# One set of input, staging and sum buffers for all stages, with each stage loading ahead for the next

## The reference

```python
h = layernorm(x)
x1 = x + cross_attention(h, ctx)            # 16 heads of 32, softmax over 154 rows
y = layernorm(x1)
for l in range(2):                          # two layers
    h = shift_token(y)                      # columns 256..511 come from the token before
    q, k, v = split(h @ wqkv[l])            # 8 heads of 64; q and k l2-normed, rotated
    y = y + local_attention(q, k, v) @ wo[l]    # window of 256, looks one window back
    h = layernorm(shift_token(y)) * lg[l] + lb[l]
    a, g = split(h @ w1[l] + b1[l])         # hidden size 1365
    y = y + (a * gelu(g)) @ w2[l] + b2[l]
return x1 + y
```

## Time and profile before

| what | value |
|---|---|
| median of 3 runs | 3664.63 us (3656.72 to 3667.29) |
| the profiled execution | 3661.59 us, its span 3659.8 us |
| mean granted clock | 0.977 |
| TensorE busy | 3448.6 us, 94% of the span |
| VectorE, ScalarE, GpSimd busy | 2278.2, 1502.2, 1138.6 us |
| DMA | 223.00 MB, 61 GB/s on average |

### The profile page before, as it was taken

How to read it: one execution, slowest core, us unless ns; L and a number is a source line. 1 busy time by engine, 2 the same in 40 slices (tenths; PEclk the granted TensorE clock), 3 DMA queues, 4 the chain that set the end, 5 groups by cost and what they waited for, 6 DMA issues and landing times. The chain is left out here.

```text
span 3659.8 us, 56458 instructions
## 1 busy us (share of the span) xinstructions
PE 3448.6 (94%) x20560; PEld 2796.4 (76%) x20560; DVE 2278.2 (62%) x5002; ACT 1502.2 (41%) x3975; POOL 1138.6 (31%) x1004
## 2 busy tenths in 40 slices
PE   5999995999999979999999979999999699999999
PEld 4667664888888867888888858888888578888887
DVE  5788875899999974333332249999999542323332
ACT  4666663555555543111111135555555321111111
POOL 2443432555565520000000035555555111111111
PEclk7999997999999999999999989999999899999999
DMA  5022224111111123111111021112111231111111
GB/s 134 14 71 63 70 60 140 47 59 59 59 59 59 59 80 96 43 43 43 43 43 43 31 95 59 59 59 69 60 60 53 88 110 48 43 38 49 47 48 37
DMA packets 201262, 223.00 MB, mean 61 GB/s; under 512 B 33286, under 2 KB 139022, under 8 KB 200987
## 3 DMA queue, kind: packets, MB, share of 16 engines
q1 hardware_dynamic: 200987, 219.38, 19.1%
HBM read 129.78 MB, written 69.64 MB: 54 GB/s over the span
## 5 line engine op out<-in xcount | busy, mean ns | idle before, releaser
L1741 DVE SCALAR_TENSOR_TENSOR u_full<-banks,b_cols,gate 128x512 f32<-128x512 f32 (+1 forms) x176 | 132.1, 751 | 888.0 <-ACT gate L1682 801.2
L46 PE MATMUL banks<-fxT_h,w_h 128*128 128x512 f32 (+1 forms) x1408 | 558.3, 396 | 8.0 <-DVE fxT_l L1733 5.0
L48 PE MATMUL banks<-fxT_h,w_l 128*128 128x512 f32 (+1 forms) x1408 | 557.4, 396 | 0.0
L47 PE MATMUL banks<-fxT_l,w_h 128*128 128x512 f32 (+1 forms) x1408 | 556.6, 395 | 0.0
L1682 ACT ACTIVATE gate<-banks,b_cols 128x512 f32<-128x512 f32 (+1 forms) x176 | 121.2, 689 | 1021.3 <-PE banks L48 1021.3
L1578 POOL TENSOR_TENSOR f_res<-f_res,b_rows 128x512 f32<-128x512 f32 x64 | 86.1, 1377 | 827.4 <-DMA f_res<-z_rows 827.4
L1027 POOL TENSOR_TENSOR rn<-ssq,neg_half 128x8 f32<-128x8 f32 x128 | 211.6, 1653 | 410.4 <-DVE ssq L1299 404.0
L46 PE MATMUL banks<-wqkv_h,hT_h 128*128 128x512 f32 x768 | 322.7, 420 | 15.1 <-DVE wqkv_l L1286 15.1
L46 PEld LDWEIGHTS banks<-fxT_h,w_h 128*128 128x128 f32 (+1 forms) x1408 | 260.4, 185 | 79.9 <-DVE fxT_l L1733 12.3
L1340 DVE TENSOR_SCALAR prob<-prob,rc 128x384 f32<-128x384 f32 (+2 forms) x512 | 315.4, 658 | 9.1
L1235 ACT ACTIVATE pT_h<-banks 128x384 fp32r<-128x384 f32 (+2 forms) x512 | 213.8, 469 | 256.0 <-PE banks L1124 254.7
(11 more groups left out here) (178 smaller groups left out, 8188.7 us busy)
## 6 DMA issues: line engine op xcount, KB each, us to landing
y_in<-y_rows SPq DMA_DIRECT2D x64, 256.0 KB, 2.9
z_rows<-y_in SPq DMA_DIRECT2D x64, 256.0 KB, 2.0
f_res<-z_rows SPq DMA_DIRECT2D x16, 1024.0 KB, 5.5
w_ffn_stage<-in_w SPq DMA_DIRECT2D x30, 512.0 KB, 5.4
x_in<-in_x SPq DMA_DIRECT2D x10, 1024.0 KB, 6.8
x_rows<-x_in SPq DMA_DIRECT2D x8, 1024.0 KB, 4.3
y_rows<-y_t SPq DMA_DIRECT2D x8, 1024.0 KB
h_in<-y_rows SPq DMA_DIRECT2D x64, 128.0 KB, 2.7
```

What stands on the lines that cost most here:

```text
L46: pe.matmul(out, a_h, b_h, start=start, stop=False)
L47: pe.matmul(out, a_h, b_l, start=False, stop=False)
L48: return pe.matmul(out, a_l, b_h, start=False, stop=stop)
L1741: e.scalar_tensor_tensor(out=u_full[r, m % 2, :], in0=ps[r, 2 * (m % 2), :], scalar=b1[r, place[m], 0:1], in1=gate[r, :], op0=ALU.add, op1 ...
```

## The change

One buffer `thirds` (three groups wide) serves as `x_in` of cross attention, and for all later stages its first two thirds are the weight stage and its last third the input tiles `h_in`. One buffer `sums` serves as `y`, `y_in` and `res`. The small tensors of the feed-forward stage are allocated once. Each stage, before it ends, issues on SP the first loads of the next: cross attention three input tiles and 4 of 8 pieces, attention group 0, four small tensors and 4 pieces, the feed-forward stage of layer 0 three tiles and 8 pieces. The statistics and the normalising of group 0 move into attention's last tile, the root to the end of GpSimd's stream. Row `N` is no longer overwritten: the store that would reach it is cut to 127 rows, once in cross attention, in each attention stage and in the feed-forward stage of layer 0. The waits for the stores at the end of a stage move to the next stage's first load of a sum. Cross attention's two unread reloads of x, the statistics of one of them, the second reload of keys and values, and the key copies of attention's last turn go. TensorE's first hidden block waits for one k of the input at a time.

```diff
+    thirds = ctx.enter_context(nc.sbuf_tensor("thirds", [P, XSLOTS, GT, D], F32))
+    stage = thirds[:, 0:2].rearrange("p s t d -> p (s t d)")
+    h_in = thirds[:, 2]
+    sums = ctx.enter_context(nc.sbuf_tensor("sums", [P, GT, D], F32))
+    X_PIECES = SLOTS["w_attn"] // 2
...
+def load_piece(e, s, w, n):
+    e.wait_ge(s["w_lo"], w.freed(n))
+    e.dma_start(w.staged(n), w.src(n)).then_inc(s["w_ld"][n % w.slots], 16)
...
 def cross_phase
-                        e.dma_start(x_in[:, g.slot(2)], src).then_inc(ld_x[g.slot(2)], 16)
+                    if it + 2 < NG:
+                        e.wait_ge(st_x1, 16 * it)
+                        e.dma_start(x_in[:, g.slot(2)], rows(io["x"], (it + 2) * G)).then_inc(ld_x[g.slot(2)], 16)
...
+                        e.dma_start(late[:, 0:GT - 1], y[:, 0:GT - 1, HALF:D]).then_inc(st_y, 16)
+                        e.dma_start(late[0:P - 1, GT - 1], y[0:P - 1, GT - 1, HALF:D]).then_inc(st_y, 16)
...
-                    if s == XSLOTS - 1:
+                    if g.it == SECOND - 1:
...
                 run(e, body)
+                e.wait_ge(st_x1, 16 * (NG - 2))
+                e.wait_ge(st_y, 32 * (NG - 3) + 16)
+                for t in range(3):
+                    load_tile(e, ahead["s"], ahead["h_in"], ahead["dram"], t)
+                e.wait_ge(st_x1, 16 * (NG - 1))
+                for n in range(ahead["pieces"]):
+                    load_piece(e, ahead["s"], ahead["w"], n)
                 store_before(Group(NG, NG, 0), NG)
                 e.wait_ge(st_x1, 16 * NG)
-                e.wait_ge(st_y, 32 * NG)
-                for s in range(XSLOTS):
-                    e.wait_ge(ld_x[s], 16 * len(range(s, NG + 1, XSLOTS)))
-                e.dma_start(dram["late"][N:N + 1, :], zero_row[:]).then_inc(st_y, 16)
-                e.wait_ge(st_y, 32 * NG + 16)
...
 def attention_phase
+                        n = P - 1 if ends_sequence(r + P) else P
+                        e.dma_start(dram["dst_late"][bass.ds(r2, n), :], y_in[0:n, j % 4, HALF:D]).then_inc(s["st"][j % 4], 16)
...
+                        if (i, u) == (0, 0):
+                            dram["is_stored"](e)
                         e.wait_ge(s["st"][u], 32 * (l * NI) + i * 32)
...
+                        if i == NI - 1 and u == 2:
+                            e.wait_ge(s["pe_h"], at(NT, NI, 4, 0))
+                            ffn_load_in(e, ahead["s"], ahead["t"], ahead["dram"], 0)
+                            ffn_load_small(e, io, ahead["s"], ahead["t"], l)
+                            e.wait_ge(w_lo, w.done(w.count))
+                            for n in range(w_next.slots):
+                                load_piece(e, ahead["s"], w_next, n)
-                        if u >= 2:
+                        if u >= 2 and i < NI - 1:
...
-                load_h(0, 0)
-                load_weights(0, w.slots)
+                load_weights(dram["pieces"], w.slots)
...
-                load_h(0, 1)
                 load_weights(w.slots, w.count)
-                load_h(0, 2)
...
                 store(NI - 1, 3)
-                e.wait_ge(s["k_copy"], 64 * (l * NI) + 64 * NI)
-                for u in range(4):
-                    e.wait_ge(s["st"][u], 32 * (l * NI) + 32 * NI)
-                e.dma_start(dram["dst_late"][N:N + 1, :], zero_row[:]).then_inc(s["ld_small"], 16)
-                e.wait_ge(s["ld_small"], 16 * 8 * l + 16 * 8)
...
                 for i in range(NI):
                     body(i)
+                ffn_root(e, ahead["s"], ahead["t"], l, 0)
...
+                        if (t, p) == (NT - 1, 0):
+                            ffn_moments(e, ahead["s"], ahead["t"], l, 0)
+                        if (t, p) == (NT - 1, 2):
+                            ffn_normalise(e, ahead["s"], ahead["t"], l, 0)
...
 def ffn_phase
-                load_in(0, None)
...
-                load_weights(0, 4 * PAIR)
+                e.dma_start(b2[:], io["b2"][bass.ds(l, 1), :].to_broadcast([P, D])).then_inc(s["ld_b2"], 16)
+                load_weights(w.slots, 4 * PAIR)
                 for g in range(NG):
+                    if is_last(g) and ahead:
+                        e.wait_ge(s["pe_x"], at(DC, NG, 0))
+                        for t in range(3):
+                            load_tile(e, ahead["s"], ahead["h_in"], ahead["dram"], t)
+                        e.wait_ge(s["w_under"], 32 * l + 32)
+                        for n in range(ahead["pieces"]):
+                            load_piece(e, ahead["s"], ahead["w"], n)
                     body(g)
-                e.wait_ge(s["st"], stored(NG))
-                if not ends:
-                    e.dma_start(dram["dst_late"][N:N + 1, :], zero_row[:]).then_inc(s["ld_small"], 16)
-                    e.wait_ge(s["ld_small"], 16 * SMALL * l + 16 * SMALL)
+                if ends:
+                    e.wait_ge(s["st"], stored(NG))
...
-                    if m == 0:
-                        e.wait_ge(s["dv_x"], at(DC, g, DC))
...
+                        if is_first(g) and m == 0:
+                            e.wait_ge(w_lo, w.done(x + 1))
                         for k in range(DC):
+                            if m == 0 and x == 0:
+                                e.wait_ge(s["dv_x"], at(DC, g, k + 1))
...
-                round_weights(0, 2)
+                round_weights(0, 1)
                 for k in range(DC):
                     affine(0, k)
-                round_weights(2, PAIR)
+                round_weights(1, PAIR)
...
-                normalise(0, lambda: rest_of_weights(0, 1))
-                rest_of_weights(1, 2)
+                rest_of_weights(0, 1)
                 for k in range(DC):
                     split_x(0, k)
-                rest_of_weights(2, PAIR)
+                rest_of_weights(1, PAIR)
```

More of the change, by code:

```diff
@@ L51, with __init__ @@
 class Pieces:
-    def __init__(self, stage, slots, pieces, l=0):
-        self.stage, self.slots, self.pieces, self.count = stage, slots, pieces, len(pieces)
+    def __init__(self, stage, slots, rows, l=0):
+        self.stage, self.slots, self.rows, self.count = stage, slots, rows, len(rows)
+        self.parts = None
         self.before = l * self.count
@@ L60, in src @@
     def src(self, n):
-        return self.pieces[n][0]
+        return self.rows[n]
     def staged(self, n):
-        shape = self.pieces[n][0].shape
+        shape = self.rows[n].shape
         at = self.stage[0:shape[0], n % self.slots, 0:int(np.prod(shape[1:]))]
@@ L395, in store_before @@
                     r, r_late = g.row(e, -1), g.row(e, -1, 1)
-                    if it is g.it and not g.last:
-                        src = rows(io["x"], (it + 2) % NG * G)
                     e.wait_ge(dv_x1, GT * it)
@@ L566, in reloaded @@
                     def reloaded(half, loaded):
[L568 to L569 removed]
+                        if it == SECOND:
+                            e.wait_ge(half, 2 * loaded)
                     for q in range(DC):
@@ L808, in body @@
                                     finish(it - 1, g.slot(-1), tt)
-                            if (q, k) in ((DC - 1, 2), (DC - 1, 4)) and not g.last:
+                            if (q, k) in ((DC - 1, 2), (DC - 1, 4)) and it + 2 < NG:
                                 moments(g.slot(2), g.round(2), (0, 1) if k == 2 else (2, 3))
-                    assert g.last or own[0] == (OWN_FIRST if g.first else OWN), own[0]
+                    assert it + 2 >= NG or own[0] == (OWN_FIRST if g.first else OWN), own[0]
                 moments(0, 0, range(GT))
@@ L849, in attention_sems, with attention_pieces, weight, load_tile @@
     return s
-def attention_phase(nc, io, ps, ident, s, neg_half, l, dram, zero_row):
+def attention_pieces(io, stage, l):
+    def weight(name):
+        src = io[name].rearrange("l k n -> (l k) n")
+        return [src[bass.ds(l * D + k * P, P), :] for k in range(DC)]
+    return Pieces(stage.rearrange("p (s d) -> p s d", d=D), SLOTS["w_attn"],
+                  [a[:, j * D:(j + 1) * D] for j in range(3) for a in weight("wqkv")] + weight("wo"), l)
+def load_tile(e, s, h_in, dram, t):
+    e.dma_start(h_in[:, t % 4, 0:HALF], dram["src"][bass.ds(t * P, P), 0:HALF]).then_inc(s["ld_h"][t % 4], 16)
+    e.dma_start(h_in[:, t % 4, HALF:D], dram["src_late"][bass.ds(t * P, P), :]).then_inc(s["ld_h"][t % 4], 16)
+def attention_phase(nc, io, ps, ident, s, neg_half, l, h_in, y_in, w, dram, ahead):
     LH = NT * HEADS
@@ L1424, in ffn_sems, with ffn_pieces @@
     return s
-def ffn_phase(nc, io, ps, ident, s, neg_half, l, dram, zero_row):
+def ffn_pieces(io, stage, l):
+    src1 = io["w1"].rearrange("l k n -> (l k) n")
+    src2 = io["w2"].rearrange("l k n -> (l k) n")
+    pieces = []
+    for c0 in range(0, HID, 2 * P):
+        n = min(2 * P, HID - c0)
+        for x in range(2):
+            pieces.append(src1[bass.ds(l * D, D), x * HID + c0:x * HID + c0 + n].rearrange("(k p) c -> p k c", p=P))
+        rows = src2[bass.ds(l * HID + c0, n), :]
```

(28 more changed lines are left out.)

200 lines of the change are left out of this document (92 added, 108 removed).

## The result

The changed kernel takes **3604.01 us** (median of 4 runs, 3602.36 to 3604.46) against 3663.23 for the kernel before (4 runs, 3656.72 to 3667.29): a ratio of 0.9839, 95% interval 0.9822 to 0.9856. That is 59 us less; 3605 was predicted, 3593 to 3618 the range. The profiled execution has a span of 3602.7 us (before 3659.8), so its 57.1 us are what the traces can account for.

A forecast was written before the change was run, and what follows sets the result against it. TensorE sets the time, so its idle waits at stage openings (38.3 and 29.7 us) can be won: 14.6 + 10.3 + 16.4 + 18.2 + 0.5 = 60.0 us off the profiled 3661.6, plus 3.0 to the median, gives 3605 us, range 3593 to 3618.

The forecast's parts named there:

- Restart: Hand-over between stages: the next stage starts 0.4 us after SP reaches its end, between 0.2 and 1.28.
- Cross attention to attention: Hand-over into attention of layer 0: 12.8 us from the earlier start plus 1.8 in the opening, 14.6 us won.
- the opening's 1.8: Attention's opening in layer 0: piece 8 issued 5.8 us after the transposes instead of 7.1, 1.8 us won in all.
- Feed-forward to attention of layer 1: Hand-over into attention of layer 1: 8.2 us from the earlier start plus 2.1 in the opening, 10.3 us won.
- Attention to feed-forward: Hand-overs into the feed-forward stage: first gate 12.5 us after the restart; net 16.4 us won in layer 0, 18.2 in layer 1.
- The 11 that I had worked out: Feed-forward opening: the second 12 matmuls end about 11 us after the restart at 2.4 GHz, about 14 at 1.2.
- The last tile: Attention's last tile: the added statistics and normalising cost 1.9 us in layer 0 and 0.5 in layer 1.
- Rest: Unread loads and one set of statistics dropped: 0.5 us won, bounds 0 to 2; the 127-row stores 0.
- the one with the clock held: Rival: shorter gaps keep the clock up, 11 us at both feed-forward openings, 9 us more won, 3596; chance 0.13.
- the other rival: Rival: low clock at feed-forward openings and a dearer last tile, where the clock falls, lose some 15 us, 3620; chance 0.13.
- The signs: Expected TensorE waits: near 2 us before the 16 transposes, 7 and 2 before attention's; first gates 14 us after attention's last matmul.
- one of the bad ones: Sign against the forecast: pieces 4 to 7 late after cross attention, behind 1.5 MB of y stores, costing up to 2 us.

The follow-up runs named there:

- the end waits back: Changed kernel with SP's wait for the landing of the last stores back at each stage's end, all loads ahead kept: 3612.62 us.
- the padding of 1696 bytes: Changed kernel with 1696 bytes of padding ahead of attention's buffers, making their shift a multiple of 2048: 3598.72 us.

## Why the prediction was right, and where it was not

**Restart, 0.4 us.** Right: 0.44 after attention, 0.65 after cross attention, 0.59 after the feed-forward stage.

**Cross attention to attention, 14.6.** Measured 12.2. The shift is right, 13.0 (609.76 to 596.76) for 12.8. The step that failed is the opening's 1.8, which came out as a loss of 0.8: from the transposes to the first residual it is 67.3 us, against 66.5 before. Piece 8 was to be issued 5.8 us after the transposes and went out after 7.5, because SP issues slower while 1.5 MB of stores are in flight. With the stores landed (the end waits back) it goes out after 5.4 and the multiply comes after 15.4 us instead of 17.1, which is 1.6 us earlier than before the change and close to what was forecast. Moving piece 8 alone could give 1.5 us at most, since the root on GpSimd is done only 1.5 us before the multiply. The other 0.6 of the loss lies between the multiply and the first residual (50.1 us, before 49.5; 49.4 to 50.5 in other executions), and its cause is open.

**Feed-forward to attention of layer 1, 10.3.** Measured 7.7: a shift of 8.0 for 8.2, and in the opening a loss of 0.3 where 2.1 were to be won. The same error: 5.5 instead of 3.8 us to piece 8, opening 65.3 us against 65.1 before. Of the 2.1 us for staged pieces 0.75 came at the multiply (14.7 us after the transposes; 15.5 before, 13.4 forecast) and were lost again before the first residual. Other executions have the multiply at 14.7 to 15.8 and an opening of 64.0 to 66.2 us, so of a gain of 2.1 there is at most half, and how much lies within that spread.

**Attention to feed-forward, 18.3 and 18.7 before the last tile's cost.** Measured 19.8 and, for layer 1, 20.2 at the first gate. The gate came 10.95 us after the restart, not 12.5. The 11 that I had worked out was right, but not as a figure for 2.4 GHz. The 1.5 us on top, a mean of the two levels because the old opening had 0.71, are a cost that isn't there: the gate comes at 10.95 us at a clock of 1.00 and of 0.84, and at 11.2 to 11.3 at 0.70. TensorE waits for VectorE and ScalarE in this opening, so the clock adds nothing at 0.84 and 0.3 us at 0.70.

**The last tile, 1.9 and 0.5.** Measured +3.6 and -0.9, together 2.7 against 2.4. As a price of the work both terms were wrong, at equal clock it is some 1.1 in each layer. Of the statistics 0.4 us reach the chain, where 0.9 and 0.5 were forecast; of the 1.92 us of normalising 0.8 reach TensorE, where it was 1.0 and 0. The difference between layers is the clock of these executions.

**Rest.** 0.5 for unread loads; not seen apart. The 127-row stores cost nothing, as forecast, though they are slow (below).

**Not in the sum.** Groups 0.3 us shorter (7 steps twice, some 4 us won) by the split-by-split wait: the line stood in the diff for every group and I had costed it only for the first. Tiles 0.08 us longer (29 steps twice, 4.4 us lost) by the addresses: moving buffers was costed at nothing. With opposite signs they left the total right by chance, as did 5 us too much for attention's openings and 3 too little for feed-forward's.

Of the rivals, the one with the clock held came nearest at the feed-forward openings: 11 us came at both, though for another reason than the clock. In the last tile the clock fell, as the other rival had it; neither case came whole. The signs hold: TensorE waits 2.0 us before the 16 transposes, 6.5 and 2.3 before attention's, on no DMA in any opening, and the first gates come 12.9 us after the last attention matmul (14 forecast). Of the signs named, one of the bad ones showed up: ScalarE waits 2.06 us on DMA for pieces 4 to 7, the price of which was inside the bounds given (0 to 2). The forecast also took the copy of 42 rows as bearing out one engine for 127 rows; nothing shows over how many engines those went, so that row says nothing of 127 rows. What runs show of those is told below.

## What to carry to other kernels

Ending a stage's queue without waiting for its last store, and having the next one's input and first weights there, is worth what stood between (8.6 us for the waits, 19 for the weights, 9 for the normalising here, each undone alone; the input ahead was not). But a load issued behind stores pays for them in its own issue and landing, so put what the opening needs first ahead of the last stores if a buffer is free (layer 1's eight pieces stand so). When buffers are merged or moved, print where the matmul operands start, and when a wait is edited inside a loop, cost it for every turn. Compare stretches at equal granted clock before giving a difference to an edit, and before pricing a low clock see whether TensorE is what the stretch waits for.

## What the runs showed of the hardware

- **Where the operands start** counts for the q, k and v projection: with attention's buffers 32 bytes off a multiple of 64 each 128x512 matmul is 2 to 3 ns longer (416 for 413, 391 for 389), 0.08 us per tile, 5 to 6 us of this kernel's time. The output projection and the product with `w2`, moved by the same 32 bytes, are not longer.
- **SP's issue of a DMA** takes 0.44 us, and 0.94 with 1.5 MB of stores in flight (1.77 and 3.75 us for four).
- **The granted clock** differs between executions of one program: over the last two tiles of attention it was 0.78 to 0.95 in profiles of the changed kernel and its edits, and 1.00 once, worth up to 5 us there (31.9 us at 1.00, 37.9 at 0.78, 0.8 of the difference being the normalising); over the feed-forward openings with all loads ahead it was 0.70 to 1.00, worth 0.3 us.
- **VectorE and GpSimd** slow each other: the subtraction with both inputs in SBUF goes from 0.6 to 1.3 us (four in 2.49 and in 5.19) beside GpSimd's rotation, while the 0.68 us multiply that reads `banks` (PSUM) keeps its time. The Trainium skill ("SBUF — State Buffer", section "Who interferes with whom") says that a VectorE instruction with two SBUF inputs contends with a GpSimd instruction that reads SBUF; the trace agrees.
- **A store of 127 rows** is slow to make way. In the middle of layer 0 (tile 15) the load issued behind it took 2.86 us to issue and 8.8 to land, against 0.45 and 2.9 behind one of 128 rows (issues view: KB, median us to landing):

```profile
1002.76 0.29 SPq L1021 DMA_DIRECT2D z_late<-sums  x1
1003.10 2.86 SPq L1031 DMA_DIRECT2D sums<-y_rows  x1
```

```profile
sums<-y_rows SPq DMA_DIRECT2D x1, 256.0 KB, 8.8
z_late<-sums SPq DMA_DIRECT2D x1, 127.0 KB
```

It is the same in layer 1 (2.72 and 8.8 us). Nobody waits there, so it costs nothing: with the padding of 1696 bytes tile 16 follows tile 15 by 18.52 us, as before the change. The Trainium skill ("DMA: Bandwidth & Descriptors", section "Why a DMA increments its semaphore by 16 and not by 1") gives 127 partitions to a single DMA engine; the trace agrees in so far as what is queued behind is late, but which engines were used was not read.
